# Attention outputs of two heads in one product, with the context halves added and the softmax division done in front of it

## The reference

```python
q = (hidden_states @ q_proj_w.T).reshape(b, s, H, Q_DIM).transpose(0, 2, 1, 3)   # H = 16 heads
...
kv = _rmsnorm(k_pass_lat, kv_a_ln_w) @ kv_b_proj_w.T                             # latent of rank 64
...
scores = jnp.where(causal[None, None], jnp.einsum(...) * scaling, NEG)
probs = jax.nn.softmax(scores.astype(jnp.float32), axis=-1)
out = jnp.einsum('bhqk,bhkd->bhqd', probs, v)
out = out.transpose(0, 2, 1, 3).reshape(b, s, H * V_DIM)
return out @ o_proj_w.T
```

## Time and profile before

| | us |
|---|---|
| median of 3 runs | 820.64 (820.28 to 822.99) |
| the profiled execution | 820.38 |
| its span, first to last instruction | 818.3 |
| around the span | 2.1 |
| attention's heads, from the first output to the last (about 82 to 408) | 326 |

### The profile page before, as it was taken

The page is one execution under the profiler, slowest core; times in us unless marked ns, Lnnn a source line. Parts: engine busy times, 40 slices in busy tenths (PEclk is TensorE's granted clock), DMA queues, the critical chain, the costliest instruction groups (busy, mean ns, idle before and its releaser), DMA issues.

```text
span 818.3 us, 16165 instructions
## 1 busy us (share of the span) xinstructions
PE 774.5 (95%) x4645; PEld 657.0 (80%) x4645; DVE 556.4 (68%) x1422; ACT 396.9 (49%) x898; POOL 271.6 (33%) x357
## 2 busy tenths in 40 slices
PE   8998989999999999999889999899989999999997
PEld 7887867777778788777779998798887778888786
DVE  5323778777878778777736666468857377777666
ACT  1234656655656566566414444313243266666531
POOL 2004446443434223231346665615423400000071
PEclk9999999999999999999999999999999999999999
DMA  7449971000000000019139899678631335555331
GB/s 213 102 109 344 404 286 42 28 28 28 28 22 22 22 22 22 21 34 333 66 98 312 300 365 353 226 280 274 240 111 61 121 99 154 155 154 154 109 97 64
DMA packets 62161, 120.74 MB, mean 148 GB/s; under 512 B 18192, under 2 KB 31760, under 8 KB 61968
## 3 DMA queue, kind: packets, MB, share of 16 engines
q1 hardware_dynamic: 51104, 95.41, 35.8%
q0 software_dynamic: 7680, 21.51, 7.3%
q10 hardware_dynamic: 3312, 3.02, 1.1%
HBM read 76.13 MB, written 43.78 MB: 147 GB/s over the span
## 4 chain that ended last, share of the span: by engine, by line
PE 72%; DVE 9%; issue 8%; POOL 5%; DMA 3%; ACT 3%; SPq 0%; DVEq 0%; ACTq 0%; POOLq 0%
PE scores L1598 9%; PE scores L1600 9%; PE scores L1599 9%; PE scores L1821 7%; PE acc_ps L2003 5%; PE misc_ps L1728 4%; PE misc_ps L1726 4%; PE probsT_ps L1713 3%; PE probsT_ps L1735 3%; PE scores L1831 3%; PE acc_ps L1713 3%; DVE xT_lo L1089 2%; POOL xd_d L770 2%; PE probsT_ps L1810 2%; DVE neg_max L1083 2%
## 5 line engine op out<-in xcount | busy, mean ns | idle before, releaser
L819 ACT ACTIVATE area<-scores,neg_max 128x128 f32<-128x128 f32 (+7 forms) x128 | 94.9, 742 | 86.5 <-DVE neg_max L1083 86.1
L1083 DVE TENSOR_REDUCE neg_max<-scores 128x1 f32<-128x128 f32 (+7 forms) x128 | 95.7, 750 | 21.9 <-PE scores L1685 21.8
L701 POOL DMA_INDIRECT xe_d<-x_rows,send_i x64 | 64.1, 1001 | 55.5 <-ACT x_rows L843 38.5
L731 POOL DMA_INDIRECT ye_d<-area,home_i x64 | 61.4, 959 | 41.2 <-issue 21.2
L1598 PE MATMUL scores<-kT_hi,weff_hi 128*128 128x512 f32 (+3 forms) x172 | 66.7, 388 | 2.2 <-issue 1.3
L1821 PE MATMUL scores<-area 128*96 128x128 f32 x512 | 66.7, 273 | 1.0 <-issue 0.6
L689 POOL CAST weff_hi<-area 128x256 fp32r<-128x256 f32 x42 | 17.0, 406 | 135.7 <-PE scores L1685 88.0
L1600 PE MATMUL scores<-kT_hi,weff_lo 128*128 128x512 f32 (+3 forms) x172 | 61.5, 358 | 0.0
L1599 PE MATMUL scores<-kT_lo,weff_hi 128*128 128x512 f32 (+3 forms) x172 | 61.5, 358 | 0.0
L1821 PEld LDWEIGHTS scores<-area 128*96 128x96 f32 x512 | 59.1, 163 | 2.1 <-issue 1.0
L776 POOL DMA_INDIRECT area<-yd_d,slot x16 | 15.2, 953 | 137.0 <-DMA yd_d<-area 132.4
(11 more groups left out here) (283 smaller groups left out, 2046.6 us busy)
## 6 DMA issues: line engine op xcount, KB each, us to landing
area<-w SPq DMA_DIRECT2D x23, 512.0 KB, 4.0
area<-gate_up SPq DMA_DIRECT2D x24, 384.0 KB, 4.5
xe_d<-area SPq DMA_DIRECT2D x8, 1088.0 KB, 11.4
area<-xe_d SPq DMA_DIRECT2D x31, 272.0 KB, 7.0
ye_d<-area SPq DMA_DIRECT2D x8, 1024.0 KB, 16.4
area<-ye_d SPq DMA_DIRECT2D x16, 512.0 KB, 5.1
area<-w SPq DMA_DIRECT2D x8, 1024.0 KB, 8.6
area<-down SPq DMA_DIRECT2D x24, 192.0 KB, 6.9
```

Source lines behind the costliest of these rows:

```text
L701: pool.indirect_dma_start(xe_d, bass.IndirectOffsetOnAxis(send_i[:, t, k:k + 1], 0), x1_rows[:, t, :], None).then_inc(sent[k % 2] if t < T ...
L819: act.activation(row_of(n)[:, 0:L], score_bank(n)[:, 0:L], ACT.Exp, bias=neg_max[:, n % 4:n % 4 + 1], accum_out=rsum[:, s, k:k + 1]).then_ ...
L1083: dve.tensor_reduce(neg_max[:, n % 4:n % 4 + 1], score_bank(n)[:, 0:(n // HEADS + 1) * P], AX.X, ALU.max, negate=True).then_inc(max_ready, 1)
```

## The change

The two halves of the context are added before the product, and the division by the row sum is done there too, so that one product can serve two heads.

- ScalarE: `swap_ctx` replaces `copy_ctx`. Two copies of 64 x 256 take the lower 64 partitions of heads 0 and 1 up, and the upper 64 partitions of heads 2 and 3 down.
- VectorE: `sum_ctx` adds each to what stayed in the bank (two additions of 64 x 256) and multiplies the result, 128 x 256, with `scale_of(G)`. The result holds heads 0 and 1 in the upper 64 partitions, and heads 2 and 3 in the lower 64. `add_group` adds one 128 x 256 result for a group to `x1`.
- GpSimd: `spread_rinv` writes the four reciprocals of a group out to 128 x 256.
- TensorE: `scale` transposes them into a bank (two transposes of 128 x 128), and `output` makes two products of 128 x 256 for a group, both summed in one bank. `wvo` holds two heads one under the other, at half its former width; the loop that fills it on VectorE copies 64 rows where it copied 128.
- The context bank is freed by `ctx_summed` (VectorE) where `ctx_copied` (ScalarE) freed it. A group has two tenants (scale at place 0, output at place 3) where it had four (an output at each odd place).
- Some semaphores are shared under new names to make room for the new ones; the waits on them have the same meaning.

```diff
+SCALE_AT, OUT_AT = 0, 3
...
-            def copy_ctx(G):
+            def swap_ctx(G):
                 act.wait_ge(ctx_step, blocks_to(G + 1))
-                if G >= 2:
-                    act.wait_ge(out_ready, QUAD * (G - 1))
-                act.copy(ctxT[:, G % 2, :], ctx_ps[:]).then_inc(ctx_copied, 1)
+                if G:
+                    act.wait_ge(ctx_summed, 2 * G)
+                act.copy(swapped[0:RANK], ctx_ps[RANK:, 0:HID]).then_inc(ctx_swapped, 1)
+                act.copy(swapped[RANK:], ctx_ps[0:RANK, HID:]).then_inc(ctx_swapped, 1)
...
+            def spread_rinv(G):
+                pool.wait_ge(rinv_done, G + 1)
+                if G >= 2:
+                    pool.wait_ge(scale_ready, G - 1)
+                pool.tensor_copy(spread[:, G % 2], rinv[:, G % 3, :].rearrange("p (m j) -> p j m", m=2).unsqueeze(3).broadcast_to(
+                    [P, 2, 2, RANK])).then_inc(rinv_spread, 1)
+
             def pool_slot(G, i, n):
+                if i == 2 and 0 <= G - 1 < GROUPS:
+                    spread_rinv(G - 1)
...
+            def sum_ctx(G):
+                for part, rows in enumerate((slice(0, RANK), slice(RANK, P))):
+                    dve.wait_ge(ctx_swapped, 2 * G + 2)
+                    dve.tensor_tensor(halves_sum[rows], ctx_ps[rows, part * HID:(part + 1) * HID], swapped[rows],
+                                      ALU.add).then_inc(ctx_summed, 1)
+                dve.wait_ge(ctx_summed, 2 * G + 2)
+                dve.wait_ge(scale_ready, G + 1)
+                if G >= 2:
+                    dve.wait_ge(out_ready, G - 1)
+                dve.tensor_tensor(pair_ctx[G % 2], halves_sum, scale_of(G), ALU.mult).then_inc(ctx_scaled, 1)
+
+            def add_group(G):
...
+                dve.tensor_tensor(x1[:, t, :], out_of(G), x1[:, t, :] if g else x_in[:, t, :], ALU.add).then_inc(out_read, 1)
...
-                behind = n - 1 - 2 * QUAD
-                if 0 <= behind < TILES * HEADS:
-                    add_head(behind)
+                if i == 0 and 0 <= G - 2 < GROUPS:
+                    sum_ctx(G - 2)
+                if i == 2 and 0 <= G - 2 < GROUPS:
+                    add_group(G - 2)
...
             def context(G, k):
...
-                        pe.wait_ge(ctx_copied, G)
+                        pe.wait_ge(ctx_summed, 2 * G)
...
+            def scale(G):
+                pe.wait_ge(rinv_spread, G + 1)
+                take_seat("scale", G)
+                for j in range(2):
+                    last = pe.transpose(scale_of(G)[:, j * P:(j + 1) * P], spread[:, G % 2, j].rearrange("p m r -> p (m r)"),
+                                        ident[:])
+                last.then_inc(scale_ready, 1)
+
+            def output(G):
+                g = G % SETS
+                pe.wait_ge(ctx_scaled, G + 1)
+                take_seat("out", G)
+                for j in range(2):
+                    last = pe.matmul(out_of(G), pair_ctx[G % 2][:, j * P:(j + 1) * P],
+                                     wvo[:, (2 * g + j) * HID:(2 * g + j + 1) * HID], start=j == 0, stop=j == 1)
+                last.then_inc(out_ready, 1)
```

More of the change, by code:

```diff
@@ L402, in build @@
         tenants = []
-        for G in range(GROUPS + 1):
+        for G in range(GROUPS + 2):
             for spot in range(8):
+                if spot == SCALE_AT and G >= 2:
+                    tenants.append(("scale", G - 2))
                 if route_at(G, spot):
@@ L407, in build @@
                 tenants += [("block", b) for b in blocks_at(G - 1, spot)]
-                if spot % 2 and 0 <= G - 2:
-                    tenants.append(("out", QUAD * (G - 2) + spot // 2))
-        tenants += [("out", QUAD * (GROUPS - 1) + i) for i in range(QUAD)]
+                if spot == OUT_AT and G >= 2:
+                    tenants.append(("out", G - 2))
         tenants += [(what, TILES - 1) for what in route_places.values()]
```

138 lines of the change are left out of this document (69 added, 69 removed).

## The result

The changed kernel takes 824.16 us (median of 20 runs, 821.71 to 828.18), the kernel before in the same company 820.57 (20 runs, 817.79 to 825.88). The ratio is 1.0045 (1.0028 to 1.0061): it is slower by 3.7 us, where 11.6 less were forecast. A second measurement beside other kernels gave 1.0033 (1.0011 to 1.0055). The profiled execution has a span of 822.4 us against 818.3, so the trace has the difference in it.

What follows compares the result with a forecast made beforehand. TensorE was taken to bound most of attention's heads, with a ScalarE-VectorE relay leading in tiles 1 and 3. Savings of 3.4 + 8.4 - 0.4 = 11.4 us gave 809.0 us, 8-in-10 range 801 to 820.5.

Steps and rivals of the forecast that it cites:

- What bounds the kernel: Attention's heads: TensorE leads in most tiles; L1735 has about 43 of its 58 us on the chain of waits.
- relay: Maximum, exp, high part, low part, next maximum between VectorE and ScalarE: 2.7 us per head with a block ahead.
- TensorE's saving: Output products and transposes: a group takes 1.12 us for 1.80, 0.68 less, so 32 groups save 21.8 us.
- The new waits on TensorE: Third block and first context of a group wait for VectorE's multiplication and additions; counted at nothing.
- No wait, with nothing to spare: Tile 7: multiplication done at about 382.9, TensorE at the block at about 383.0; waits of L1754 on L1136 would show error.
- ScalarE: Two copies, 0.74 us, replace one of 0.58 ahead of exp; exp and the first addition some 0.05 late.
- VectorE: Four operations for four per group, 0.43 us each, bounds 0.27 and 0.6; load stays, the place changes.
- The lump just fits: The three `sum_ctx` operations, 1.4 us at a group's start, fit 1.82 us in tile 7 and 1.40 in tile 3.
- The rival "slower": `sum_ctx` sits in the relay, for instance at 0.6 us per operation: 16 us lost against 11.4 gained, 825; 13 in 100.
- GpSimd: Spread of reciprocals, 0.41 us each, 13 us in all; 0.4 lost at the end, between 0 and 1.
- The clock: Rival: more waiting lets TensorE's clock fall to 1.2 GHz, in one tile costing as much as the change gives; 2 in 100.
- The sum: 3.4 us from tile 0 and last group, 8.4 from 20 groups, nothing from tiles 1 and 3, 0.4 lost at end.

Runs made afterwards that it cites:

- e5_noswap: Changed kernel without ScalarE's two copies; the additions wait for the last context itself and read memory set once: 814.18 us, ratio 0.9920 to before.
- e6_nowait: Changed kernel with both ScalarE copies reading ready memory and nobody waiting for them: 853.54 us beside 864.44 of before on another chip, ratio 0.9883.
- e4_nomult: Changed kernel without VectorE's multiplication by the reciprocals; the additions write what the output reads: 821.87 us, ratio 1.0011 to before.
- e1_out5: Changed kernel with the output product at place 5 for 3 and add_group one slot later: 818.24 us, ratio 0.9976 to before.
- e11_after: The changed kernel once more, unchanged, beside before on another chip: 824.36 us, ratio 1.0033.
- e8_onecopy: Changed kernel with late output, multiplication parted from additions in short tiles, and one 64x512 copy for two: 848.64 us beside before's 864.44, ratio 0.9827; repeated 0.9899.

## Why the prediction was wrong, point by point

**What bounds the kernel.** The reading of the chain was right in its parts: relay in tiles 1 and 3, TensorE elsewhere. What it missed is how little TensorE led. Three quarters of L1735 on the chain was read as "time of the kernel", but a line's share of the chain says what it costs now, not what comes back when it is gone; the next limit lay a few tenths behind.

**TensorE's saving.** The mechanism was right, and so was the size: 128 records of the output product where 256 stood, and two transposes of the reciprocals 0.21 us ahead of the next work (382.60 to 382.81 in tile 7). Where the two products of a group do not wait, the chain has them at 0.86 us, 0.43 each, inside the 0.43 to 0.49 that were counted:

```profile
250.19 0.86 PE probsT_ps L1785 x4
```

The busy time fell by less than the 21.8 us counted, by 10.8 in the heads and by 8.2 over the span, but busy time is modelled.

**The new waits on TensorE** were "counted at nothing". This is the first step that failed. The working followed the third block and the first context, in one group of tile 7, and never the output itself at place 3, in any tile. The output waits for the multiplication behind the whole chain of copies, additions and VectorE's queue. Moving it two places gave 4.3 us in tiles 1 to 7, 1.1 in tile 0 and 0.9 in the tail, the clock's falls among them. The wait of a block for the multiplication was forecast as "No wait, with nothing to spare" and came in 8 groups, 4.5 us: 2.85 us in three groups where the router's product stands ahead and shifts the banks by one, which the working did not count, and 1.6 us in five groups without it. It was one of the prediction's own signs of being wrong.

**ScalarE.** This is the second step that failed. The durations were right (0.37 each, 0.74 for 0.58). "Exp is some 0.05 late" is right for tile 7 and was taken for all. In the short tiles the copies stand in ScalarE's queue ahead of an exp that could already run, as in the group at 85.78. The term was mis-sized: the copies cost 9.0 us in tiles 1 to 7 (e5_noswap), 3.0 by the wait for them and at most 6.0 by ScalarE's time (e6_nowait), and a single copy gets 3.5 of them back. The 9.0 and the 4.3 of the output's place can't be added, since the output waits for the same chain.

**VectorE.** Operations of 64 partitions take 0.42, inside 0.27 to 0.6 and at the value taken. "The lump just fits" was nearly right: without the multiplication only 2.0 us come back (e4_nomult), and parting it helps tiles 1 and 2 by 1.5 us and hurts the long ones. The rival "slower" had the right sign and nearly the right time (825), but for another reason than its example: operations of 0.6 did not come. Its general condition, copies and operations together longer than the stretch, did hold in the short tiles: from 85.78 to 87.90 they take 2.1 us where 1.4 were counted as free. And the low parts were late all the same, since the lump began late, behind the copies, as in the group at 86.57.

**GpSimd.** The spread takes 0.40, and no wait of TensorE in the heads is put down to GpSimd. In the tail it had 0.85 us to spare at 412.48; the 0.4 counted for it was not lost there. The tail's 0.84 us has three parts. 0.42 lie between the last reciprocal and the last context (3.69 us where it was 3.27), at a granted clock of 1.00; with the output two places later it is 3.22 (e1_out5), so they are the output's place. 0.18 lie between the last context and the statistics (4.38 us where it was 4.20), and 0.23 between the power on GpSimd and the first send, with the clock down in a part of both.

**The clock** had 2 in 100, on the ground that it was 1.00 in all windows of before. Its falls are part of the loss in both traces of after: some 0.4 and 0.6 us in the tail, by the same stretches of e1_out5 (4.23 us where after has 4.38 and e11_after 4.81, and 5.64 from the power to the first send where they have 5.90 and 5.64), and in tile 1 some part of the 2.4 us by which that tile is longer than before (group 6 has 8.45 us in after and 7.98 in e4_nomult without a fall).

**The sum.** Forecast was 8.4 us from 20 groups that TensorE leads, 3.4 from tile 0 and the end, nothing from tiles 1 and 3. Measured by the trace: +3.35 from tiles 4 to 7, -1.5 from tile 0, -4.3 from tiles 1 to 3 (-0.9 of it in tile 2, whose four groups were counted among the 20), -0.84 in the tail. That something is lost lay with a rival that had 13 in 100, and its 825 is close by luck: it was made of 16 us lost and 11.4 gained. "I count nothing" for the relay's tiles was too kind: work put into a relay is a loss there, not a nought. With the output late, the lump parted in the short tiles and one copy, the change gives 8.3 us; that is another order than the one that was forecast.

## What to carry to other kernels

An operation that is moved ahead of a consumer in an in-order queue has to be placed by when its input is ready, in the shortest stage as well as in the longest: walk the whole chain, copies and hand-offs, to the product that ends it, before counting a new wait at nothing. Where the work passes between engines like a relay, an engine at 49% can be on the path for a part of the time: of some 10 us of copies that were added there in the old order about 2 came through in tiles 1 to 7, and of some 4 us that were taken away in the changed one (e8_onecopy) 3.5. Freeing the busiest engine gives back only the slack to the relay. When a change frees an engine but comes out slower, try its places in the order first; here two numbers were worth 5.7 us, more than the loss.

## What the runs showed of the hardware

- A copy by ScalarE from PSUM of 64x512 takes 582 ns, as 128x512 does (583); 64x256 takes 365 to 370, as 128x256 does. An addition by VectorE of 64x256 with one operand in PSUM takes 415 to 422 ns, and 128x256 in SBUF and PSUM 421. Half the partitions save nothing.
- TensorE's granted clock was at its lower level around 76 to 86 us in one execution of the kernel before and not in another, at a cost of 3.2 us. Other falls came within 2 us after TensorE had stood for about 2 us (from about 110 and 411 us in after), but waits as long in e4_nomult (2.3 us) and e1_out5 (1.99 us) had none behind them there.
- On one chip what follows attention took some 35 us longer than on the others, while attention's tiles agreed within 0.1 us.
